# Where VectorE makes its last choice, where the third product is copied, and a new order of splits, norms and loads around the pairs of key tiles

## What is computed

```python
def _L0_attn_ref(x, w_gate, w_up, w_down):          # x: 1024 rows of 512, I = 1376
    s = silu(einsum('bsh,ih->bsi', x, w_gate))
    k = int(0.5 * I)
    _, idx = top_k(-abs(s), k)                      # the 688 smallest of each row ...
    s = s with s[row, idx] = 0                      # ... become zero
    s = s * einsum('bsh,ih->bsi', x, w_up)
    return einsum('bsi,hi->bsh', s, w_down)

def _L0_xattn_ref(hidden_states, cross_attention_states, mask, Wq, Wk, Wv, Wo, ...):
    k = cross_attention_states @ Wk.T               # 6404 keys, 8 groups of 128
    v = cross_attention_states @ Wv.T
    k = rmsnorm(k) per group of 128
    ...                                             # softmax attention, 32 heads
```

## Time and profile before

| | us |
|---|---|
| median of 3 runs | 2756.97 (2756.02 to 2757.91) |
| the profiled execution, its own time | 2755.8 |
| its span in the trace | 2754.0 |
| PE busy | 2676.1 |
| DVE busy | 2147.3 |
| ACT busy | 1601.2 |
| POOL busy | 1370.8 |

### The profile page before, as it was taken

One profiled execution on the slowest core, in us unless ns is written; L12 is line 12 of the kernel. 1 busy time (PEld: TensorE's weight loads), 2 busy tenths in 40 slices (PEclk: granted clock), 3 DMA queues, 4 the chain that ended last, 5 costly groups with the idle time before them and its releaser, 6 DMA issues.

```text
span 2754.0 us, 47471 instructions
## 1 busy us (share of the span) xinstructions
PE 2676.1 (97%) x14454; PEld 2317.5 (84%) x14454; DVE 2147.3 (78%) x3162; ACT 1601.2 (58%) x3660; POOL 1370.8 (50%) x1232
## 2 busy tenths in 40 slices
PE   9989999986999999999999999999999999999999
PEld 8877777764878888888888888888888888888887
DVE  5899999997065558888888888888888888888544
ACT  3276666653523446666666666666666666666421
POOL 0277777787213346555555555555555555554000
PEclk9999999998999999999999999999999999999999
DMA  6423334332452444211111111211121211112532
GB/s 221 131 77 114 114 114 114 114 108 75 126 187 93 129 130 125 65 57 63 56 50 60 55 60 57 63 57 63 57 63 57 63 57 63 57 44 85 181 115 73
DMA packets 260695, 247.31 MB, mean 90 GB/s; under 512 B 13232, under 2 KB 215728, under 8 KB 260624
## 3 DMA queue, kind: packets, MB, share of 16 engines
q1 hardware_dynamic: 260624, 246.45, 29.0%
HBM read 150.55 MB, written 95.85 MB: 89 GB/s over the span
## 4 chain that ended last, share of the span: by engine, by line
PE 79%; POOL 10%; issue 6%; ACT 4%; DVE 1%; DMA 1%; POOLq 0%; SPq 0%; ACTq 0%; DVEq 0%
PE banks L162 21%; PE banks L163 21%; PE banks L164 21%; PE banks L2178 13%; POOL v_sb L769 2%; POOL rstd L749 2%; POOL s_lo L766 2%; ACT square L846 2%; ACT k_sb L856 1%; POOL u L769 1%; POOL c_lo L741 1%; PE banks L1685 1%; PE banks L2195 1%; POOL s_sum L757 1%; PE banks L2193 1%
## 5 line engine op out<-in xcount | busy, mean ns | idle before, releaser
L2134 DVE TENSOR_TENSOR pT_lo<-banks,pT_hi 128x512 fp32r<-128x512 f32 (+1 forms) x832 | 573.1, 689 | 93.2 <-ACT pT_hi L2053 80.6
L2053 ACT CAST pT_hi<-banks 128x512 fp32r<-128x512 f32 x576 | 334.5, 581 | 405.9 <-PE banks L2178 405.6
L977 DVE TENSOR_SCALAR_CACHE_REDUCE flags<-abs_s,thr 128x1376 bf16<-128x1376 f32 x256 | 403.7, 1642 | 1.1
L162 PE MATMUL banks<-k_hi,q_hi 128*128 128x416 f32 (+1 forms) x1024 | 374.3, 365 | 0.1
L163 PE MATMUL banks<-k_lo,q_hi 128*128 128x416 f32 (+1 forms) x1024 | 352.6, 344 | 0.0
L164 PE MATMUL banks<-k_hi,q_lo 128*128 128x416 f32 (+1 forms) x1024 | 350.7, 343 | 0.0
L162 PE MATMUL banks<-pT_hi,v_hi 128*128 128x512 f32 x768 | 344.2, 448 | 0.0
L1945 POOL TENSOR_SCALAR p_even<-p_even,p_inv 128x1601 f32<-128x1601 f32 x127 | 205.5, 1618 | 262.3 <-DVE p_inv L2093 262.1
L2086 DVE CUSTOM_DVE_ANT_0 p_odd<-banks,minus_mask 128x1664 f32<-128x1664 f32 x128 | 242.1, 1892 | 89.0 <-PE banks L164 89.0
L163 PE MATMUL banks<-pT_lo,v_hi 128*128 128x512 f32 x768 | 302.2, 394 | 0.0
L164 PE MATMUL banks<-pT_hi,v_lo 128*128 128x512 f32 x768 | 302.1, 393 | 0.0
(11 more groups left out here) (244 smaller groups left out, 6323.9 us busy)
## 6 DMA issues: line engine op xcount, KB each, us to landing
raw<-keys SPq DMA_DIRECT2D x32, 800.5 KB, 4.6
keys<-kT_sb SPq DMA_DIRECT2D x50, 512.0 KB, 4.9
values<-v_sb SPq DMA_DIRECT2D x50, 512.0 KB, 3.5
raw<-values SPq DMA_DIRECT2D x32, 768.0 KB
queries<-qT_sb SPq DMA_DIRECT2D x64, 256.0 KB, 2.6
raw<-queries SPq DMA_DIRECT2D x32, 512.0 KB, 5.3
attended<-o_sb SPq DMA_DIRECT2D x128, 128.0 KB, 1.9
raw<-attended SPq DMA_DIRECT2D x64, 256.0 KB, 2.9
```

The costliest lines, as they stand in the source:

```text
L162: pe.matmul(out, a_hi, b_hi, start=start, stop=False)
L977: bits.done(dve.tensor_scalar(flags[:, tt % 2], abs_s[:, tt], thr[:, tt:tt + 1].bitcast(F32), 0.0, ALU.is_lt, ALU.add, accum_out=out[:, tt ...
L2053: act.copy(pT_hi[:, m % RING], t_bank(m)).then_inc(pT_hi_act, 1)
L2134: dve.tensor_tensor(pT_lo[r, m % RING], t_bank(m)[r], pT_hi[r, m % RING].bitcast(F32), ALU.subtract).then_inc(pT_lo_done, 1)
```

## The change

It does six things, all in `keys_and_values`:

1. The sums of value weights T1 to T4 were made half by VectorE (k = 0) and half by GpSimd (k = 1). Now VectorE makes all eight, behind the split of B11, and `sum_weights` is gone.
2. ScalarE's start of the stage has another order: input tile 2 is split first, then the three blocks that need no sum, then the squares of tile 0 (into `first_square`, which waits for one store in place of two), the sums' blocks, the norm of tile 0, the squares of tile 1.
3. P7 is copied to `v_sb[:, 1, left]` in place of `u[:, 1]`. ScalarE no longer waits for GpSimd's first addition (`U2`) before it; it waits for `U3` before the copy of P4 instead.
4. Block B12 is split inside the last pair, before the squares of tile 42, on ScalarE and on GpSimd.
5. VectorE waits for B12's low half before the first `choose`.
6. SP takes down's first loads one tile earlier in its queue (`LAST - 2`), and the left-over keys' stores go behind the last tile; GpSimd does their norms at tile 48.

```diff
-    t_sum0_done, t_sum1_done = sem("w_lo_done"), sem("x_lo_done")
+    t_sum_done = sem("w_lo_done")
...
-    V_ITEMS = [(B11, R11), (T2, None), (T3, None), (T1, None), (B21, R21), (T4, None), (B22, R22)]
+    V_ITEMS = [(B11, R11), (B22, R22), (B21, R21), (T1, None), (T2, None), (T3, None), (T4, None)]
...
+    LO_ORDER = [B11, T2, T3, T1, B21, T4, B22]
...
-            if t == LAST - 1:
-                sp.wait_ge(chosen, t_sum0(5))
+            if t == LAST - 2:
+                sp.wait_ge(chosen, t_sum_at(T_SUMS) + 1)
...
+        rest.sync(sp)
 
     def gpsimd(pool):
...
             pool.wait_ge(v_sb_done, copied(p, P7_SB))
-            add(u[:, 1], u[:, 0], u[:, 1])
+            add(u[:, 1], u[:, 0], v_sb[:, 1, left])
...
             split_c(i, s + 4)
+            if is_last(i, s):
+                split_b12()
             root(i, s + 2)
...
-        for m in range(4):
-            wait_v_raw(pool, 1, m)
-        pool.wait_ge(sem("u_done"), done(TT - 1))
-        sum_weights(pool, 1, t_sum1_done, t_sum1)
...
+            if t == LAST - 1:
+                rest.gpsimd(pool)
...
             take(p, P6, u[:, 1], b_ps)
-            act.wait_ge(u_sum_done, u_sum(p, U2))
-            take(p, P7, u[:, 1], e_ps)
             act.wait_ge(v_out[1], landed(p - 1))
+            take(p, P7, v_sb[:, 1, left], e_ps)
             take(p, P5, v_sb[:, 1, right], d_ps)
...
+            act.wait_ge(u_sum_done, u_sum(p, U3))
             take(p, P4, v_sb[:, 1, left], e_ps)
...
             split_c(i, s + 4)
+            if is_last(i, s):
+                split_b12(act)
             squares(i, s + 2)
             norm_keys(i, s + 2)
...
-        split_value_weights(V_ITEMS[:1])
+        split_c(0, 2)
+        split_value_weights(V_ITEMS[:3])
+        act.wait_ge(sem("p_out0"), landed(TT // 2 - 1))
+        squares(0, 0, first_square)
+        split_value_weights(V_ITEMS[3:6])
+        norm_keys(0, 0)
         act.wait_ge(sem("p_done"), done(TT - 1))
...
+        split_v(B11)
+        sum_v(T1, R12, R11, None)
+        sum_v(T2, R22, None, T1)
+        sum_v(T3, R22, R12, None)
+        sum_v(T4, R21, None, T2)
+        for blk in LO_ORDER[1:]:
+            split_v(blk)
...
+        dve.wait_ge(w_lo_done, CHUNKS + 2 * PRODUCTS + 2)
         for t in range(TT):
             for part in range(4):
                 choose(t, part)
```

More of the change, by code:

```diff
@@ L534, in keys_and_values @@
     square = [chip.at(f"square{h}", [P, 512], place + 2 * N) for h, place in enumerate((AT_S, AT_P))]
+    first_square = [chip.at(f"first_square{h}", [P, 512], AT_P + 512 * h) for h in range(2)]
     v_sb = chip.at("v_sb", [P, 2, N], AT_S)
@@ L561, in keys_and_values, with t_sum_at @@
     GATE_W = 2 * GB + 2 * CT - 2
-    t_sum0_done, t_sum1_done = sem("w_lo_done"), sem("x_lo_done")
+    t_sum_done = sem("w_lo_done")
     s_sum_done, s_hi_done, s_lo_done = sem("x_lo_done"), sem("x_hi_done"), sem("w_hi_done")
     u_sum_done, chosen = sem("table_done"), sem("w_lo_done")
-    def t_sum0(n):
+    def t_sum_at(n):
         return GATE_W + n
-    def t_sum1(n):
-        return done(TT - 1) + 4 + n
     def s_sum_at(p, n):
-        return done(TT - 1) + 4 * p + n + (4 if not isinstance(p, int) or p else 0)
+        return done(TT - 1) + 4 * p + n
     def s_hi_at(p):
@@ L654, in keys_and_values @@
     R11, R12, R22, R21 = range(4)
-    V_ITEMS = [(B11, R11), (T2, None), (T3, None), (T1, None), (B21, R21), (T4, None), (B22, R22)]
+    V_ITEMS = [(B11, R11), (B22, R22), (B21, R21), (T1, None), (T2, None), (T3, None), (T4, None)]
+    T_SUMS = 8
+    HI_OF = {blk: n for n, (blk, m) in enumerate(V_ITEMS)}
+    LO_ORDER = [B11, T2, T3, T1, B21, T4, B22]
+    SUM_OF = {T1: 0, T2: 1, T3: 2, T4: 3}
     def v_source(blk, m, k):
@@ L792, in window, with split_b12 @@
             split_c(i, s + 4)
+            if is_last(i, s):
+                split_b12()
             root(i, s + 2)
+        def split_b12():
+            for k in range(2):
+                pool.wait_ge(w_hi_done, CHUNKS + 2 * PRODUCTS + k + 1)
+                pool.tensor_tensor(vw[:, B12, 1, k], vw_full[:, B12, 1, k], vw[:, B12, 0, k].bitcast(F32), ALU.subtract
+                                   ).then_inc(w_lo_done, 1)
         pool.wait_ge(sem("rest_products"), 2 * G * REST)
@@ L807, in gpsimd @@
         pairs(pool, window)
[L808 to L812, removed]
         pool.wait_ge(v_done, product_done(PAIRS, 0))
@@ L838, in split_s, with squares @@
             act.copy(s_hi[:], s_sum[:]).then_inc(s_hi_done, 1)
-        def squares(i, s):
+        def squares(i, s, into=square):
             t = BODY * i + s
@@ L845, in squares @@
                 at = slice(g * HD, (g + 1) * HD)
-                last = act.activation(square[g // 4][:, g % 4 * HD:(g % 4 + 1) * HD], k_banks(s)[:, at], ACT.Square,
+                last = act.activation(into[g // 4][:, g % 4 * HD:(g % 4 + 1) * HD], k_banks(s)[:, at], ACT.Square,
                                       accum_out=ssq[:, s % RING, g:g + 1])
@@ L869, in window @@
             p = pair(i, s)
-            squares(i, s + 1)
             act.wait_ge(u_sum_done, u_sum(p, 0))
@@ L888, in window, with split_b12 @@
             split_c(i, s + 4)
+            if is_last(i, s):
+                split_b12(act)
             squares(i, s + 2)
             norm_keys(i, s + 2)
+            if not is_last(i, s):
+                squares(i, s + 3)
+        def split_b12(act):
+            for k in range(2):
+                act.wait_ge(w_in[SLOTS - 2 + k], 32)
+                act.copy(vw[:, B12, 0, k], vw_full[:, B12, 1, k]).then_inc(w_hi_done, 1)
         def split_value_weights(items):
@@ L895, in split_value_weights @@
                     if m is None:
[L896 removed]
+                        act.wait_ge(t_sum_done, t_sum_at(2 * SUM_OF[blk] + k + 1))
                     else:
@@ L910, in scalar @@
         split_s(0)
-        split_value_weights(V_ITEMS[:1])
-        act.wait_ge(sem("p_done"), done(TT - 1))
[L913 to L919, removed]
+        split_c(0, 2)
[4 more added lines that the diff above has]
+        norm_keys(0, 0)
+        act.wait_ge(sem("p_done"), done(TT - 1))
+        act.wait_ge(sem("p_out1"), landed(TT // 2 - 1))
+        squares(0, 1)
+        split_value_weights(V_ITEMS[6:])
         pairs(act, window)
-        for k in range(2):
-            act.wait_ge(w_in[SLOTS - 2 + k], 32)
-            act.copy(vw[:, B12, 0, k], vw_full[:, B12, 1, k]).then_inc(w_hi_done, 1)
         for t in range(FIRST, LAST):
@@ L962, in vector, with split_v, sum_v @@
         dve.wait_ge(sem("u_done"), done(TT - 1))
[L963 to L966, removed]
+        chunk_of = dict(V_ITEMS)
+        def split_v(blk):
             for k in range(2):
-                dve.wait_ge(w_hi_done, CHUNKS + 2 * n + k + 1)
-                dve.tensor_tensor(vw[:, blk, 1, k], v_source(blk, m, k), vw[:, blk, 0, k].bitcast(F32), ALU.subtract
-                                  ).then_inc(w_lo_done, 1)
+                dve.wait_ge(w_hi_done, CHUNKS + 2 * HI_OF[blk] + k + 1)
+                dve.tensor_tensor(vw[:, blk, 1, k], v_source(blk, chunk_of[blk], k), vw[:, blk, 0, k].bitcast(F32),
+                                  ALU.subtract).then_inc(w_lo_done, 1)
+        def sum_v(blk, a, b, ready):
+            for k in range(2):
+                first = v_raw(k, a)
+                second = v_raw(k, b) if ready is None else vw_full[:, ready, 1, k]
+                wait_v_raw(dve, k, a)
+                if ready is None:
+                    wait_v_raw(dve, k, b)
+                else:
+                    dve.wait_ge(t_sum_done, t_sum_at(2 * SUM_OF[ready] + k + 1))
+                dve.tensor_tensor(vw_full[:, blk, 1, k], first, second, ALU.subtract).then_inc(t_sum_done, 1)
+        split_v(B11)
[5 more added lines that the diff above has]
+            split_v(blk)
         bits = Chain(dve, chain)
```

1 line of the change is left out of this document (removed).

## The result

The changed kernel takes 2689.16 us (median of 4 runs, 2688.24 to 2689.72), against 2757.44 us (4 runs, 2756.02 to 2759.25) for the kernel before on the same chip: ratio 0.9752, 95% interval 0.9735 to 0.9769, so 68.3 us saved. The forecast was 2683, its range 2676 to 2698. The profiled execution took 2689.7, 66.1 us less than that of before, where the sum said 73.9.

What follows compares the result with a forecast made beforehand. PE was taken as the bound, half idle from 593 to 670 while VectorE chooses; savings of 9.3 + 15.4 + 21.8 + 17.2 + 2.2 + 8 = 73.9 us gave 2681.9 profiled, 2683 us median, range 2676 to 2698.

Steps and rivals of the forecast that it cites:

- (b): Twenty pairs: P7's copy no longer waits for U2, each pair shrinks by 0.77 us, 15.4 us saved; bounds 0 to 17.
- (c): Last two pairs: VectorE waits instead of choosing, so GpSimd is not stretched; 21.8 us saved, bounds 19 to 22.
- (d): B12 before values of tile 42: PE waits 2.4 us in place of 19.4; 17.2 us saved, bounds 16 to 19.
- (f): Down's start: PE's wait for VectorE's gating, held up by its load, goes away; 8 us saved, up to 8.6.
- (a): Stage start: B11's split comes first, P4 of pair 0 starts earlier; 9.3 us saved, bounds 7 to 10.
- GpSimd, which loses its four sums, is idle then: Step at the stage's start: GpSimd idle, so 9.3 us was taken rather than 7 for sums at half pace.
- (e): Values of tile 42 and keys of 43: full clock expected after 2.4 us idle; 2.2 us saved, bounds 0 to 2.2.
- the low half of the input that GpSimd splits behind its sums takes the wait's place: Rival in the pairs: this split, or another copy, keeps the loop's length, the 15.4 us saving becomes 0: 2698; chance 0.09.
- Slow choices: Rival: the eight choices, moved beside later tiles, still take 77.1 us and delay down's loads: 10 us back, 2693; chance 0.15.
- Roots late in the tail: Rival in the tail tiles: GpSimd's root instructions, stretched by VectorE, come late for PE; chance 0.08.
- the worst case: Late tail roots, stretched 5.4 us against 5.1 us of slack: 0.3 us in each of five tiles, 1.5 us.
- the 14 us of a wait for whole instructions every time: Late tail roots, each root instruction waiting for a whole 3.99 us scan: PE loses 2.9 us a tile, 2697.

Runs made afterwards that it cites:

- the run with GpSimd waiting: Changed kernel, but at the stage's start GpSimd does tile 0's root and tile 2's split only behind VectorE's low half of T2: 2697.12 us.
- the second execution: The changed kernel profiled again, unchanged, as a control on the same chip as later edits; that measurement took 2691.23 us.
- the root first: Changed kernel with GpSimd's root of tile s+2 ahead of the split of tile s+4, in all pairs but the last: 2686.45 us.
- both edits: Changed kernel with GpSimd's root ahead of its input split and B12's loads ahead of the last pair's first key store: 2683.52 us, ratio 0.9728.

## Why the prediction was right, and where it was short

**Right in mechanism and place.** (b), (c), (d) and (f) each have an experiment that undoes one part: +15.4 (P7's place), +19.3 (VectorE's wait), +7.5 (B12's place), +7 to +12 (the loads' place). For (a) there is only the sharing of the sums, worth 1 to 3 us; what B11's split ahead of the sums and ScalarE's new order gave is not shown by a run of its own, nor is the new place of the left-over keys. (c) came out exact: VectorE counted until 585.8, waited 26 us, and nothing stretched GpSimd in the pairs. In (f) no wait is left at the gates. The loads are issued at 675.66, later than the 673.8 that I named as the limit, and still PE does not wait: the first gating starts at 690.46, 8.2 us before PE arrives, and PE itself arrived 7.7 us later than forecast (698.70 for 691.0). That is luck: with the 17.2 us that I took from load to restart, a PE that had come at 691.0 would have waited for 1.9 us.

The bounds of (a) to (f), each at its best, add up to 78.8 us, so the time could have been 2678 at the least, and not 2676; each at its worst, with 8 for (f), they give 2707, above the range. Its ends are a judgement and not a sum.

**(a) 5.0 for 9.3: the step that failed is "GpSimd, which loses its four sums, is idle then".** It is not. It splits the input sums beside B11's split (1.93 in place of 1.28) and splits input tile 2 beside T4's sums (2.37 in place of 1.28). That is 1.7 us, of which the run with GpSimd waiting took back 1.1. The first of the two could be seen in the kernel before, whose GpSimd does that split until 133.69, while the sum took B11's split to start at 132.92:

```profile
131.28 2.41 POOL L766 TENSOR_TENSOR s_lo<-s_sum,s_hi 128x1024 fp32r<-128x1024 f32 x1 [1.83 <-DVE kw_lo L957]
```

The remainder differs between executions of one kernel: in the profiled one the stage began 1.0 us later (B11's split at 133.93 for 132.92), and after PE's wait of 2.24 the granted clock was 0.60 in the next 4 us, which cost 1.6. In the second execution it was 1.00, though PE waited 2.26; there the mark is 148.90, a gain of 7.3, and 1.7 and a start 0.3 late make up what is missing of 9.3. My lower bound of 7 was the better value, and 5.0 lies below even that. I had read half pace from the 1.31 us of the first sum of before; the three behind it took 1.66 to 1.78. In the end the slow matmuls cost nothing: at pair 20 the two executions are 0.7 us apart, which is what their starts differ by, since GpSimd's loop sets the pair. The Trainium skill, page "SBUF — State Buffer", section "Who interferes with whom", has the rule that fits: a VectorE instruction with two SBUF inputs contends with a GpSimd instruction that reads SBUF, for ports that one of them holds exclusively, and the order of issue decides who is held up. The trace agrees on both sides, with the 3.43 us of a 0.20 us instruction of GpSimd and with VectorE's 2.37 for 1.28.

**(b) 14.5 for 15.4.** The loop was named rightly, and its length was short by what stays between U2 and U3: I took away all of the 0.77 us, but 0.15 is left, mostly U2's own end. 23.12 less 0.62 is 22.50, and from pair 7 to 20 a pair takes (599.12 - 306.71) / 13 = 22.49 us. In the seven ahead of them, where the loop does not hold PE up yet, it is 22.22. The mean is 22.40, and 22.48 in the second execution; with the root first it is 22.27. The rival "the low half of the input that GpSimd splits behind its sums takes the wait's place" names where the loop now meets PE: I gave it 0.09 as one that takes everything, and it took 0.13 to 0.21 us a pair, 2.6 to 4.2 in all. That it hangs on GpSimd's order is shown by putting the root first.

**(d) and (e) 16.0 and 0.8 for 17.2 and 2.2.** B12's loads landed 4.9 to 5.4 us after their issue, and the two issues took 2.19 us of SP's queue together; from the mark to the values it is 12.8, not 11.6. Loading earlier gives just the 11.6. After the 3.57 us of idle PE ran at half clock for a while: the granted clock was 0.62 in the next 4 us, and its first matmul took 0.77. In the kernel that loads B12 first it was 1.00 after 2.33 us of idle, and the first matmul took 0.47, as I had expected for 2.4.

**The rivals that stayed away.** Slow choices: 63.8 us, even 2.8 below the forecast 66.6. Roots late in the tail: the six tail tiles took 70.7 us as before, with no wait. One root was stretched to 4.30 us there and its slack hid it; in the second execution of the same kernel PE waited 1.5 us once (for a norm, at 638.2), the size that I had called the worst case, and far from the 14 us of a wait for whole instructions every time.

## What to carry to other kernels

When two engines stretch each other's instructions, look which of them PE waits for, and let the other one rest: one wait on VectorE, which had 26 us to spare, was worth 30 of 68 us. When a wait of PE is removed, work out the loop through the other engines first; here it left 0.1 to 0.2 us a pair, and the idle time of the engine that closes the loop told which instruction to move up (4.8 us for one line). An engine called idle in a sum must be looked up instruction by instruction in that very stretch, and a small instruction held back on it can cost more than the large ones that it made room for.

## What was not expected of the hardware

- `var`, 128x8, takes GpSimd 0.20 us and took 3.43 beside six VectorE splits of 0.60 in a row. Beside the counting, which reads one tensor, the 36 splits of the input that GpSimd did from 165 to 580 took 1.30 us in the mean, where B12's two, with VectorE idle, took 1.26 each.
- After idle time at one and the same place (before the values of tile 42) the clock fell or held without regard to its length. The windows of the next 4 us, first of the kernel with both edits (idle 1.86), then of that with the root first (3.34); the granted clock stands behind the engines:

```profile
605.97:609.97 4.00, 4.00 (x11) 3.14 (x12) 3.93 (x3) 0.34 (x3) 3.38 (x2) 0.57 0.52 170
```

```profile
607.00:611.00 4.00, 4.00 (x18) 3.29 (x19) 3.93 (x3) 0.01 (x1) 3.72 (x2) 1.00 0.65 202
```

  It was 1.00 also after 2.33 and 3.75 us, and 0.62, 0.50 and 0.57 after 3.57, 3.81 and 4.50 (0.50 is the lower level, 1.2 GHz). The 48 matmuls that follow took 11.0 us where it held and 12.4 to 13.3 where it fell. What decides it is open.
- The program's first loads, which are the same in both kernels, did not always land alike: the four of `abs_s` took 9.9 us (median) in the profiled execution of before and 11.0 in that of the changed kernel, where the stage began 1.0 us later; in the second one it was 10.1, and the stage began 0.3 later. That the one caused the other is likely and not shown.
- A choice took VectorE 7.40 us where GpSimd worked not at all beside it (619.21 to 626.61), and 7.41 beside a root that itself was stretched from 1.64 to 4.30; beside a split of the input and a root it took 8.42 (626.61 to 635.03). In these rows the small root waits for VectorE and does not slow it; the split does.
